# Sixteen-head attention steps: the order of probability transposes and V products, and the copies of groups 1 and 3

## The reference

```python
# _L1_xattn_ref: queries from x (normalised), keys and values from ctx (120 keys)
Q = proj(q, w_q); K = proj(k, w_k); V = proj(v, w_v)       # 16 heads of 8
scores = einsum('bhsd,bhtd->bhst', Q, K) * D_K ** (-0.5)
attn = softmax(where(mask == 0, MASK_VALUE, scores), axis=-1)
x = einsum('bhst,bhtd->bhsd', attn, V)                     # heads joined
x + einsum('bsd,ed->bse', x, w_o)
# _mla, in _L1_ffn_ref: the same over x itself (128 keys, causal), k and v through a 64-wide latent
```

## Time and profile before

| what | value |
|---|---|
| median of 3 runs | 1313.48 us (1313.0 to 1314.64) |
| the profiled execution, its own time | 1314.13 us |
| its span, first to last instruction | 1311.9 us |
| mean granted TensorE clock | 0.972 |
| busy: PE, PEld, DVE, ACT, POOL | 93%, 67%, 71%, 61%, 45% |

### The profile page before, as it was taken

How to read it: one execution, slowest core, us unless ns; L and a number is a source line. 1 busy time by engine, 2 the same in 40 slices (tenths; PEclk the granted TensorE clock), 3 DMA queues, 4 the chain that set the end, 5 groups by cost and what they waited for, 6 DMA issues and landing times. The chain is left out here.

```text
span 1311.9 us, 37944 instructions
## 1 busy us (share of the span) xinstructions
PE 1224.1 (93%) x13719; PEld 876.5 (67%) x13719; DVE 925.8 (71%) x2003; ACT 795.9 (61%) x2101; POOL 588.4 (45%) x673
## 2 busy tenths in 40 slices
PE   1799999999999995996999999999999979999996
PEld 0466666666666663444888788878888857777775
DVE  6377667767766774565999999999999955333431
ACT  0577887887788783223878778766666623333332
POOL 3577656665665664303333433353333234333343
PEclk9899999999999998995999999999999989999998
DMA  7100000000000000000000002000000000000000
GB/s 211 22 1 2 0 0 0 0 0 0 0 0 0 0 1 1 0 0 11 12 8 9 10 11 72 3 3 2 0 0 0 1 1 9 9 8 8 8 14 12
DMA packets 22743, 14.75 MB, mean 11 GB/s; under 512 B 6378, under 2 KB 21610, under 8 KB 22540
## 3 DMA queue, kind: packets, MB, share of 16 engines
q1 hardware_dynamic: 22520, 13.75, 3.9%
q10 hardware_dynamic: 148, 0.01, 0.0%
HBM read 11.66 MB, written 2.10 MB: 10 GB/s over the span
## 5 line engine op out<-in xcount | busy, mean ns | idle before, releaser
L690 POOL TENSOR_TENSOR r_norm<-ssm,mhalf 128x24 f32<-128x24 f32 x32 | 134.8, 4214 | 163.0 <-DVE ssm L595 163.0
L1767 POOL TENSOR_TENSOR pair_QX<-pair_qT,own_slots 128x512 f32<-128x512 f32 x64 | 66.6, 1041 | 249.2 <-ACT pair_qT L1579 234.4
L1985 ACT ACTIVATE moe_hid<-psum 128x512 f32<-128x512 f32 x128 | 76.3, 597 | 136.9 <-PE psum L1919 136.9
L1525 PE MATMUL psum<-ident,pair_probs 128*120 128x128 f32 (+1 forms) x1024 | 153.7, 283 | 0.7 <-ACT pair_probs L1594 0.6
L533 ACT ACTIVATE l_probs<-psum,l_n_max 128x248 f32<-128x248 f32 x256 | 117.0, 481 | 57.5 <-DVE l_n_max L613 57.5
L2143 POOL TENSOR_TENSOR moe_acc<-moe_acc,moe_prod 128x512 f32<-128x512 f32 x64 | 81.4, 1272 | 146.6 <-DVE moe_prod L2099 146.6
L1594 ACT ACTIVATE pair_probs<-psum,pair_n_max 128x120 f32<-128x120 f32 (+1 forms) x512 | 137.3, 379 | 11.3 <-DVE pair_n_max L1636 6.0
L1929 PEld LDWEIGHTS psum<-w,moe_hid 128*128 128x128 f32 x1024 | 123.2, 192 | 26.8 <-issue 26.8
L2099 DVE TENSOR_TENSOR moe_prod<-psum,moe_combine 128x512 f32<-128x512 f32 x64 | 44.2, 691 | 135.1 <-PE psum L1929 135.1
L1525 PEld LDWEIGHTS psum<-ident,pair_probs 128*120 128x120 f32 (+1 forms) x1024 | 109.3, 141 | 31.5 <-ACT pair_probs L1594 12.8
L1462 ACT COPY pair_probsT<-psum 120x512 f32<-120x512 f32 (+1 forms) x128 | 78.7, 614 | 84.9 <-PE psum L1525 84.9
(11 more groups left out here) (292 smaller groups left out, 2917.8 us busy)
## 6 DMA issues: line engine op xcount, KB each, us to landing
X<-x_in SPq DMA_DIRECT2D x8, 256.0 KB, 5.4
out_dram<-moe_acc SPq DMA_DIRECT2D x32, 64.0 KB, 1.5
CT<-ctx_in SPq DMA_DIRECT2D x8, 240.0 KB, 5.7
pair_cT<-ctxT_in SPq DMA_DIRECT2D x32, 60.0 KB, 1.8
w<-w_in SPq DMA_DIRECT2D x1, 1024.0 KB, 5.1
wm<-wm_in SPq DMA_DIRECT2D x1, 768.0 KB, 4.5
wp<-wp_in SPq DMA_DIRECT2D x1, 768.0 KB, 6.7
wkv<-wkv_in SPq DMA_DIRECT2D x1, 512.0 KB, 5.1
```

The lines of the kernel that those rows point to most:

```text
L690: pool.tensor_tensor(r_norm[:, :], ssm[:, :], mhalf[:, 0:3 * H], ALU.pow).then_inc(s["norm_inverted"], 1)
L1525: tr = pe.transpose(psum[0:K, 4 + g % 2, j * P:(j + 1) * P], probs[par][:, 4 * g + j, 0:K], ident[:, :])
```

## The change

Only the order of calls in three `body` functions of `attentions16` changes, with one copy that goes from DVE to ACT. On PE, group 3 is turned after `project`, q, k and v come next, then group 2; the four calls of `multiply_v` follow in a row; groups 1 and 0 of the next entry are both turned after `scores`. On ACT, group 1 is now copied ahead of group 0, and `exp_a` moves over the border between two bodies and is cut in half with `copy_q` between the halves; it also waits for group 0 to be turned, since that is now the last of the two. On DVE, the copy of group 1 goes, and the copy of group 3 moves from before `max_b` to after `shift_b`.

```diff
 PE      def body(n, par, k, l1=None):
-                    turn_group(n - 1, 1 - par, 3, l1)
                     turn_input(n + 1)
                     project(n - 2, l1)
+                    turn_group(n - 1, 1 - par, 3, l1)
+                    project_qkv(n + 1, 1 - par, l1)
                     turn_group(n - 1, 1 - par, 2, l1)
-                    project_qkv(n + 1, 1 - par, l1)
                     multiply_v(n - 1, 1 - par, 0, l1)
                     multiply_v(n - 1, 1 - par, 1, l1)
-                    turn_group(n, par, 1, l1)
                     multiply_v(n - 1, 1 - par, 2, l1)
                     multiply_v(n - 1, 1 - par, 3, l1)
...
                     scores(n + 1, 1 - par, l1)
+                    turn_group(n, par, 1, l1)
                     turn_group(n, par, 0, l1)
 ACT
-                def exp_a(n, par, l1):
+                def exp_a(n, par, l1, some):
...
                         wait(act, turned[1], n - 1)
-                        for h in range(8):
+                        wait(act, turned[0], n - 1)
+                        for h in some:
...
-                        e.then_inc(a_exp_done, 1)
+                        if some.stop == 8:
+                            e.then_inc(a_exp_done, 1)
...
                 def body(n, par, k, l1=None):
+                    exp_a(n, par, l1, range(0, 4))
                     copy_q(n + 1)
+                    exp_a(n, par, l1, range(4, 8))
                     copy_group(act.copy, act, n - 1, 2, l1)
                     copy_k(n + 1, 1 - par, l1)
...
+                    copy_group(act.copy, act, n, 1, l1)
                     copy_group(act.copy, act, n, 0, l1)
-                    exp_a(n + 1, 1 - par, l1)
 DVE
                     copy_input(dve, n + 1, l1)
-                    copy_group(dve.tensor_copy, dve, n - 1, 3, l1)
                     add_projection(n - 2, l1)
                     max_b(n, par, l1)
+                    shift_b(n, par, l1)
+                    copy_group(dve.tensor_copy, dve, n - 1, 3, l1)
                     take_stats(n - 2, l1)
-                    shift_b(n, par, l1)
...
-                    copy_group(dve.tensor_copy, dve, n, 1, l1)
                     copy_values(dve.tensor_copy, dve, n + 1, 1 - par, l1)
```

## The result

| what | before | changed |
|---|---|---|
| median | 1314.06 us (1313.0 to 1315.41) | 1333.1 us (1332.19 to 1334.23) |
| ratio | | 1.0143, 95% interval 1.0128 to 1.0158 |
| profiled execution, its own time and span | 1314.13, 1311.9 us | 1332.19, 1328.2 us |
| mean granted clock | 0.972 | 0.975 |

The change costs 19 us, where 22 was forecast (1336, range 1324 to 1343). The kernel is slower although DVE lost a copy in each step and TensorE's products with V stand in one run.

The account below looks back on a forecast made before the run. PE was taken to set the pace, with ACT and DVE practically tied. Steps 0.355 (cross) and 0.385 us (self attention) longer, plus 0.2 for the held-up step, gave 22.1 on the median of 1313.48: 1336 us, range 1324 to 1343.

Parts of the forecast that it names:

- What bounds the kernel now: Sixteen-head stage: PE sets the pace, ACT only 0.04 us behind, DVE with 0.04 a step left; three chains tied.
- lengthening any one costs nearly in full: Sixteen-head stage: with PE, ACT and DVE chains tied, any lengthening of one shows almost wholly in the step time.
- The rest of the loop costs what it did: PE outside the stretch from q, k and v to the third multiply_v call: same instructions, same wait for ACT, unchanged time.
- ACT, the second copy: ACT copies group 1, then group 0 0.46 us later, so the exponentials of half a start 0.22 later.
- ACT, q in the middle: Between the exponential halves ACT stands from 904.58 to 904.72, waiting for q, k and v on PE.
- The new stretch: End of q, k and v on PE to third multiply_v call: 1.915 us against 1.53 in self attention, 0.385 more a step.
- DVE, the copy of group 3: Behind shift_b on DVE, needed by the fourth multiply_v call: hidden, or late by 0.1 us at worst.
- The sum: Sixteen-head stage: 29 x 0.355, 30 x 0.385 and 0.2 for the held-up step, together 22.1 us more.
- q does not hold ACT up: Rival: exponentials run on past q on ACT, only the second copy costs, 0.23 us a step, 1327 us; chance 0.12.
- PE's saving comes through: Rival: group 2's copy is ready when PE arrives, saving 0.18 to 0.34 us a step, 1293 to 1303 us; chance 0.08.
- The clock: Rival: transposes in runs, then PE pauses, lower the clock, about 1419 us; chance 0.03, shared with another late wait above 1343.
- What would show it: Signs: PE idle 0.5 to 0.7 us before the third call, ACT idle some 0.15 ahead of q, DVE near 85%.

Follow-up runs that it names:

- that run: Kernel before, with ACT instead of DVE copying group 1, ahead of the exponentials of half b: 1311.25 us, ratio 0.9985.
- the last run above: Changed kernel, group 2 turned early and copied before q between the exponential halves, group 3 copied before shift_b, search's matmul one step later: 1296.48 us, ratio 0.9856.

## Why the prediction was right, point by point

- **What bounds the kernel now** (three tied chains, PE's own gaps first): held. With DVE at 91% the steps of before stay at 6.74. That "lengthening any one costs nearly in full" is too broad: ACT took a copy more in that run and the step stayed, since the copy stood outside the chain.
- **The rest of the loop costs what it did**: held. From the third call to the next mask products it is 1.01 before and after, and from there to the end of q, k and v on PE 4.20 both times (904.68 - 900.48 and 970.95 - 966.75).
- **ACT, the second copy**: forecast 0.22 later for the exponentials. It was 969.87 - 966.75 = 3.12 after the mask products against 2.87, so 0.25.
- **ACT, q in the middle**: forecast a stand of 0.14. Four exponentials from 969.87 on would be through at 970.88, and q started at 970.98: 0.10. Part of that comes back, since the copy of group 2 took 0.61 in the changed kernel and 0.67 where q stands last. Undoing it gave 0.07 in the cross attention, and in the self attention too once DVE's copy was out of the way (7.08 to 7.01). So this term was sized at double its worth: of the 0.385 the forecast gave 0.23 to the second copy and 0.155 to q, and the runs give 0.26 and 0.07.
- **The new stretch**: 1.915 forecast, 1.87 measured in the self attention (0.03 + 0.17 + 1.00 + 0.61 + 0.06), the copy of group 2 being the term that was too long by 0.04. In the cross attention 0.355 more was forecast and 0.33 came.
- **DVE, the copy of group 3**: "hidden, or late by 0.1 at worst". It was ready 0.05 ahead of the fourth call, and became the bound, by 0.03, as soon as q was moved.
- **The sum**: 22.1 forecast for the stage, 17.4 measured between its first and last mask products. The 59 regular steps cost 19.2, the held-up step 0.2 (7.88 to 8.07), the first two 0.4 together. "The first two, the last and the one where moments delay the cross attention I leave as they are" was the term that failed: the one with the moments saved 2.3 us. Of these, 1.07 come up to the start of q, k and v (740.75 - 736.11 = 4.64 after the mask products, against 5.71). The copy of group 1 that no longer stands ahead of the moments on DVE has the main part of that; moved alone, it gave 0.60. The other 1.22 come behind, where the clock of before was down. That the median came so near, 19 us above the old one, is partly luck: the two profiled executions differ by 18.1 in their own time but by only 16.3 from first to last instruction (outside the stage 1.1 came back), and no row shows what the other 1.8 are.
- **Rivals**: "q does not hold ACT up" would have been 1327, and the run that moved q back gave 1328. "PE's saving comes through" named 0.18 to 0.34 a step, and the runs that freed the copy of group 2 show 6.75 - 6.49 = 0.26. The gain was there, hidden behind ACT, though those runs also turn group 2 right behind group 3, which the forecast order does not. The clock stayed at 1.00 in the regular steps, with 17 transposes in each. The Trainium skill says in TensorE: Matmul & The Clock Gate, Part 4, that transposes don't count as activity the way products do; these steps, where products stand among them, show no effect of that.
- **What would show it**: PE's wait ahead of the third call came as named (0.70 on the weight loads). The idle time ahead of q did not appear as such, and by the letter of its last sentence the forecast would have been wrong by that; the stand of 0.10 is there all the same, so the sign was badly chosen. The record of the last exponential of the first half ends at 969.87 + 1.16 = 971.03, after q's start at 970.98, so the profile counts no idle time there. Only the spacing shows it: q normally starts 0.16 before that end (905.36 against 903.35 + 2.17). DVE's share of 85% was 89%, which fits neighbours that wait and so no longer overlap, but was not looked into.

## What to carry to other kernels

When several engines are within a few hundredths of each other, a busy share of 99% says nothing about what a relief is worth: follow the chain once around the loop and add up what the change puts into it. A shorter order on one engine pays only if the operand that it now asks for earlier is also made earlier; here 19 us of loss became 10 us of gain once group 2 was turned earlier and the copy that PE waits for went ahead of half the work in front of it. Before judging a version by its first bound, look for the second one right behind it.

## What was not expected of the hardware

A pause of PE seems to cost more than its length here. In the moments step of before, PE waited 1.60 us for DVE's input copy and 0.80 for its scaled output, and the products with V right after took 0.65 to 0.66 us in place of 0.42: the granted clock was at its lower level there (0.50 from 738.20 to 740.00, 0.85 over the step). In the changed kernel the wait for the input copy was 1.15, the clock stayed at 1.00, and the same products took 0.43. The obvious reading is that the longer pause let the clock fall. Two other runs speak against a rule that simple. In the last run above no wait of that step was longer than 0.87, and yet the clock fell (0.83 over the step, weight loads of 0.41 in place of 0.24). With group 1 copied by ACT in the kernel before, waits of 0.41, 0.43 and 1.15 add up to about the same as the last run's 0.87, 0.42 and 0.68, and the clock stayed at 1.00. What decides stays open; no run varied the pause by itself, and each kernel shows it in one profiled execution only. Rows of the step: kernel before, changed kernel, last run.

```profile
736.97 0.30 PEld L1493 LDWEIGHTS psum<-pair_zT,l_wq 128*128 128x128 f32 x2 [1.60 <-DVE pair_zT L1453]
...
738.26 0.66 PE L1536 MATMUL psum<-pair_probsT,V 120*32 120x128 f32 x8
```

```profile
740.75 0.30 PEld L1493 LDWEIGHTS psum<-pair_zT,l_wq 128*128 128x128 f32 x2 [1.15 <-DVE pair_zT L1453]
...
742.04 0.43 PE L1536 MATMUL psum<-pair_probsT,V 120*32 120x128 f32 x8
```

```profile
725.83:735.74 9.91, 8.58 (x141) 6.94 (x137) 8.44 (x26) 7.74 (x21) 4.43 (x5) 0.83 0.04 9
```

```profile
729.11 0.30 PEld L1547 LDWEIGHTS psum<-l_wo,pair_outT 128*128 128x128 f32 x2 [0.87 <-DVE pair_outT L1673]
...
731.40 0.30 PEld L1493 LDWEIGHTS psum<-pair_zT,l_wq 128*128 128x128 f32 x2 [0.68 <-DVE pair_zT L1453]
...
733.30 0.41 PEld L1536 LDWEIGHTS psum<-pair_probsT,V 120*32 120x32 f32 x8
```
